# Ranks of layer 1's tokens from shifted products with the matrix of ones, without sums on GpSimd

## The reference, cut to what matters

```
def _L1_ffn_ref(x, gate_w, w1, w2, w3):
    xf = x.reshape(-1, orig_shape[-1])
    scores = jnp.einsum('td,ed->te', xf, gate_w)
    probs = jax.nn.softmax(scores.astype(jnp.float32), axis=-1)
    weights, idx = jax.lax.top_k(probs, TOP_K)          # TOP_K = 2 of 8
    weights = weights / jnp.sum(weights, axis=-1, keepdims=True)
    x1 = jax.nn.silu(jnp.einsum('td,efd->tef', xf, w1))
    x3 = jnp.einsum('td,efd->tef', xf, w3)
    out_all = jnp.einsum('tef,edf->ted', x1 * x3, w2)
    expert_outs = jnp.take_along_axis(out_all, idx[:, :, None], axis=1)
    result = jnp.einsum('tkd,tk->td', expert_outs, weights)
...
xn = _layernorm(x, axis=-1)
x = x + _L1_attn_ref(xn, ...) + _L1_ffn_ref(xn, L1_ffn_gate_w, L1_ffn_w1, L1_ffn_w2, L1_ffn_w3)
```

## Time and profile before

| | us |
|---|---|
| median of 3 runs | 1725.74 |
| lowest, highest | 1725.56, 1727.15 |
| span of the profiled execution (first to last instruction) | 1724.1 |
| TensorE busy in it | 1679.7 (97%) |
| VectorE, ScalarE, GpSimd busy | 1350.6, 812.6, 609.5 |

### The profile page before, as it was taken

The page is one execution under the profiler, slowest core; times in us unless marked ns, Lnnn a source line. Parts: engine busy times, 40 slices in busy tenths (PEclk is TensorE's granted clock), DMA queues, the critical chain, the costliest instruction groups (busy, mean ns, idle before and its releaser), DMA issues.

```text
span 1724.1 us, 24432 instructions
## 1 busy us (share of the span) xinstructions
PE 1679.7 (97%) x7020; PEld 1188.6 (69%) x7020; DVE 1350.6 (78%) x3866; ACT 812.6 (47%) x1456; POOL 609.5 (35%) x656
## 2 busy tenths in 40 slices
PE   5999999999999999999999999999999999999995
PEld 4667777777777777777777777777777766667773
DVE  5878888888888787979797979787888776565558
ACT  4535453636363545454544445454545343554431
POOL 3311242424242324233333232332323233567770
PEclk8999999999999999999999999999999999999998
DMA  8949474646373747373737373645546445577758
GB/s 211 201 104 256 100 187 105 178 109 181 99 181 101 182 103 194 97 200 86 202 84 192 85 189 90 174 106 135 144 106 167 99 109 154 191 266 266 237 173 312
DMA packets 172339, 273.89 MB, mean 159 GB/s; under 512 B 14312, under 2 KB 57320, under 8 KB 171952
## 3 DMA queue, kind: packets, MB, share of 16 engines
q1 hardware_dynamic: 163632, 254.63, 56.1%
q0 software_dynamic: 8576, 17.70, 3.2%
HBM read 202.15 MB, written 65.93 MB: 155 GB/s over the span
## 4 chain that ended last, share of the span: by engine, by line
PE 94%; DVE 2%; ACT 1%; issue 1%; DMA 1%; POOL 0%; SPq 0%; POOLq 0%; DVEq 0%; ACTq 0%
PE ps_y L709 26%; PE ps_gate L660 8%; PE ps_gate L661 8%; PE ps_gate L662 8%; PE ps_up L662 8%; PE ps_up L660 8%; PE ps_up L661 8%; PE ps_y L735 4%; PE ps_side L675 3%; PE ps_side L758 1%; PE ps_side L852 1%; PE ps_side L835 1%; PE ps_side L794 1%; PE ps_side L819 1%; PE ps_side L660 1%; PE ps_side L661 1%
## 5 line engine op out<-in xcount | busy, mean ns | idle before, releaser
L918 DVE TENSOR_TENSOR silu_h<-ps_up,silu_h 128x512 f32<-128x512 f32 x618 | 424.0, 686 | 295.3 <-ACT silu_h L1325 243.3
L1325 ACT ACTIVATE silu_h<-ps_gate 128x512 f32<-128x512 f32 x618 | 367.6, 598 | 567.4 <-PE ps_gate L662 565.1
L709 PE MATMUL ps_y<-silu_h,w_dn 128*128 128x512 f32 x1056 | 542.7, 595 | 3.0 <-DVE silu_h L912 3.0
L912 DVE TENSOR_TENSOR silu_h<-coef_b,silu_h 128x512 f32<-128x512 f32 x528 | 386.8, 732 | 13.0 <-DMA coef_b<-coef_kept 9.2
L660 PE MATMUL ps_gate<-xnT,w_gu 128*128 128x512 f32 x528 | 342.7, 649 | 0.0
L709 PEld LDWEIGHTS ps_y<-silu_h,w_dn 128*128 128x128 f32 x1056 | 199.7, 189 | 53.7 <-issue 7.7
L660 PE MATMUL ps_up<-xnT,w_gu 128*128 128x512 f32 x528 | 207.9, 394 | 4.6 <-DVE silu_h L918 4.6
L661 PE MATMUL ps_gate<-xnT,w_gu 128*128 128x512 f32 x528 | 209.4, 397 | 0.0
L662 PE MATMUL ps_gate<-xnT,w_gu 128*128 128x512 f32 x528 | 208.9, 396 | 0.0
L662 PE MATMUL ps_up<-xnT,w_gu 128*128 128x512 f32 x528 | 208.0, 394 | 0.0
L661 PE MATMUL ps_up<-xnT,w_gu 128*128 128x512 f32 x528 | 206.8, 392 | 0.0
(11 more groups left out here) (267 smaller groups left out, 2454.8 us busy)
## 6 DMA issues: line engine op xcount, KB each, us to landing
coef_b<-coef_kept SPq DMA_DIRECT2D x254, 512.0 KB, 6.8
slots_x<-empty SPq DMA_DIRECT2D x15, 2080.0 KB, 12.7
w_block<-w_kept SPq DMA_DIRECT2D x45, 512.0 KB, 3.9
xs<-slots_x SPq DMA_DIRECT2D x37, 260.0 KB, 3.8
y_back<-y_kept SPq DMA_DIRECT2D x15, 512.0 KB, 7.0
w_down<-in_ffn_w SPq DMA_DIRECT2D x45, 128.0 KB, 3.7
w_raw<-in_ffn_w SPq DMA_DIRECT2D x33, 128.0 KB, 7.9
xres<-in_x SPq DMA_DIRECT2D x16, 256.0 KB, 3.1
```

The costliest lines, as they stand in the source:

```text
L709: eng.matmul(ps_y[:, :], w_dn[:, j], silu_h[:, g % HBUFS], start=j == 0, stop=last).then_inc(pe_down)
L912: eng.tensor_tensor(silu_h[:, s], coef_b[:, q % COEF_RING, k], silu_h[:, s], ALU.mult).then_inc(dve_h)
L918: eng.tensor_tensor(silu_h[:, s], ps_up[g % 2][:, :], silu_h[:, s], ALU.mult).then_inc(dve_h1)
L1325: eng.activation(silu_h[:, s], ps_gate[g % 2][:, :], ACT.Silu).then_inc(act_silu)
```

## The change

"prefix" goes from both tables and from GpSimd, and `gbefore` and its semaphore `pool_before` with it. "rank" on TensorE now has five products in place of two: the one with `neg_before` as before, and four with `neg_ones`, each reading `gsel` from its first block on and writing the bank from block 1, 2, 3 and 4 on: 32, 24, 16 and 8 columns. What lands in a block is the sum over all blocks in front of it. "rank" no longer waits for GpSimd. "select" on VectorE, before it overwrites `gsel`, now waits until the "rank" of the chunk before has read it; GpSimd had that wait before, for `gbefore`.

```diff
@@ ROUTE1 and ROUTE1_LAST
-          (31, "prefix"), (39, "rank"), (40, "key"), ...
+          (39, "rank"), (40, "key"), ...
-               (16, "prefix"), (17, "rank"), (18, "key"), ...
+               (17, "rank"), (18, "key"), ...
@@ build_program
-        gbefore = sb("gbefore", [ROWS + 1, EXPERTS1])
@@ tensor, "rank"
                     eng.wait_ge(dve_sel, key + 1)
-                    eng.wait_ge(pool_before, (ROWS + 1) * (key + 1))
-                    eng.matmul(ps[:, 0:(ROWS + 1) * EXPERTS1], neg_before, flat(gsel[:, :, :]), start=True, stop=False)
-                    eng.matmul(ps[:, 0:(ROWS + 1) * EXPERTS1], neg_ones, flat(gbefore[:, :, :]), start=False, stop=True).then_inc(signal)
+                    wide = (ROWS + 1) * EXPERTS1
+                    eng.matmul(ps[:, 0:wide], neg_before, flat(gsel[:, :, :]), start=True, stop=False)
+                    for back in range(1, ROWS + 1):
+                        ins = eng.matmul(ps[:, back * EXPERTS1:wide], neg_ones, flat(gsel[:, 0:ROWS + 1 - back]), start=False, stop=back == ROWS)
+                    ins.then_inc(signal)
@@ vector, "select"
                     wait_own()
+                    if c > 0:
+                        eng.wait_ge(*done("rank", min(c, SPARSE) - 1))
                     eng.tensor_scalar(gsel[:, 0:ROWS], gleft[:, :, :], CHOSEN, None, ALU.is_le).then_inc(dve_sel)
@@ gpsimd
-                elif what == "prefix":
-                    ...
-                            eng.tensor_copy(gbefore[:, 1], gsel[:, 0]).then_inc(pool_before)
-                    ...
-                            eng.tensor_tensor(gbefore[:, r + 1], gbefore[:, r], gsel[:, r], ALU.add).then_inc(pool_before)
```

More of the change, by code:

```diff
@@ L78 @@
 ROUTE1 = [(5, "stats1"), (7, "norm1"), (8, "xT1"), (9, "x_lo1"), (10, "vl0"), (10, "vl1"), (11, "top1"), (12, "gate_exp"), (23, "softmax"), (30, "select"),
-          (31, "prefix"), (39, "rank"), (40, "key"), (41, "first2"), (42, "slot"), (43, "send0"), (45, "send1"), (47, "send2"), (48, "send3"),
+          (39, "rank"), (40, "key"), (41, "first2"), (42, "slot"), (43, "send0"), (45, "send1"), (47, "send2"), (48, "send3"),
           (49, "send4"), (51, "send5"), (53, "send6"), (54, "send7")]
 ROUTE1_LAST = [(5, "stats1"), (7, "norm1"), (8, "xT1"), (9, "x_lo1"), (10, "vl0"), (10, "vl1"), (11, "top1"), (12, "gate_exp"), (14, "softmax"), (15, "select"),
-               (16, "prefix"), (17, "rank"), (18, "key"), (19, "first2"), (20, "slot"), (20, "table"), (21, "send0"), (21, "send1"), (22, "send2"), (22, "send3"),
+               (17, "rank"), (18, "key"), (19, "first2"), (20, "slot"), (20, "table"), (21, "send0"), (21, "send1"), (22, "send2"), (22, "send3"),
                (23, "send4"), (23, "send5"), (24, "send6"), (24, "send7")]
@@ L363, in build_program @@
             sem(n) for n in ("act_kexp", "act_qexp", "act_qrelu", "dve_kfeat", "pool_qfeat"))
-        dve_gate, act_gate, dve_sel, dve_slot, dve_gw, dve_gates, pool_mark, pool_before, dve_logit1, dve_strike1, act_attend, dve_sum, act_keys = (
-            sem(n) for n in ("dve_gate", "act_gate", "dve_sel", "dve_slot", "dve_gw", "dve_gates", "pool_mark", "pool_before", "dve_logit1",
+        dve_gate, act_gate, dve_sel, dve_slot, dve_gw, dve_gates, pool_mark, dve_logit1, dve_strike1, act_attend, dve_sum, act_keys = (
+            sem(n) for n in ("dve_gate", "act_gate", "dve_sel", "dve_slot", "dve_gw", "dve_gates", "pool_mark", "dve_logit1",
                                  "dve_strike1", "act_attend", "dve_sum", "act_keys"))
@@ L1537, in step @@
                     eng.tensor_tensor(qf[:, :], qf[:, :], tmp0[:, :], ALU.add).then_inc(pool_qfeat)
-                elif what == "prefix":
[L1540 to L1548, removed]
-                            eng.tensor_copy(gbefore[:, 1], gsel[:, 0]).then_inc(pool_before)
-                        else:
-                            eng.wait_ge(pool_before, (ROWS + 1) * c + r + 1)
-                            eng.tensor_tensor(gbefore[:, r + 1], gbefore[:, r], gsel[:, r], ALU.add).then_inc(pool_before)
                 elif what.startswith("put"):
```

## The result

The changed kernel takes 1745.28 us (median of 4 runs, 1744.72 to 1745.75) where the kernel before takes 1725.86 (1725.56 to 1727.15): 19.4 us more, a ratio of 1.0112 with a 95% interval of 1.0100 to 1.0124. The prediction was 1735.1 us in a range of 1731 to 1739. The direction was right; the size was half of what came, outside the range.

A forecast was written before the change was run, and what follows sets the result against it. TensorE, busy 97% of the span, was taken as the bound: 9.9 us of added products less 0.5 us of wait gave +9.4 on 1724.1, 1733.5, plus 1.6 to the runs' median: 1735.1 us, range 1731 to 1739.

The forecast's parts named there:

- What bounds the kernel: At the ranks, TensorE alone is late, busy 893.00 of 893.00 us; anything between two tiles moves the end by its length.
- The price of the added products: At each rank on TensorE, three more float32 products of 0.22 us: 0.66 us, 9.9 us over 15 ranks.
- the rival in which a narrow product costs only its columns: At the ranks, 0.07 us more each, 1.0 us for 15, less 0.5: +0.5, 1726.2 us; chance 0.05.
- The wait at chunk 14: TensorE's rank at chunk 14 no longer waits for GpSimd's sums: 0.5 us come back, once.
- the rival that the wait was dearer than it is booked: 8.1 us of idle time before L825's weight loads goes too: +1.8 us, 1727.5 us; chance 0.04.
- GpSimd's sums and VectorE's wait at zero: Work leaving GpSimd gives nothing; VectorE's added wait before writing gsel has 66 us of slack and costs zero.
- The rival in which the sums hold VectorE back: GpSimd's 1.8 us of sums delay VectorE and TensorE follows: 27 us gained, 1708 us in all; chance 0.04.
- The stall behind chunk 14: After chunk 14's routing, VectorE waits 3.94 us for an indirect send, then TensorE waits; it moves with TensorE, giving nothing back.
- The clock: TensorE's clock falls near chunk 14's stall cost 3.4 us; as before 0.74, otherwise 0.13 (-3.4 to +3.4, 1731.7 to 1738.5 us).
- 9.9 - 0.5 = +9.4 us: Whole kernel: added products at 15 ranks less the wait at chunk 14, on the 1724.1 us span: 1733.5 us.
- a chunk longer by another amount with the same number of passes: Sign of being wrong: a full chunk grows by something other than 0.66 us though TensorE's passes are as forecast.

The follow-up runs named there:

- three_more: Kernel before, GpSimd's sums and places kept, plus three products with neg_ones at each rank into unread columns: 1786.96 us against 1777.38.
- ranks16: Changed kernel with 160 free bytes where gbefore stood and the five rank products in bfloat16: 1721.28 us against 1726.13, ratio 0.9973.
- kept_third: Changed kernel with 160 bytes per partition held free where gbefore stood, third run: 1735.41 us against 1725.98 for the kernel before, ratio 1.0056.
- keep_place: Changed kernel with 160 bytes per partition held free where gbefore stood, first run: 1785.32 us against 1777.38 for the kernel before.
- before16: Kernel before, GpSimd's sums and places kept, with its two rank products in bfloat16: 1721.84 us against 1726.13, ratio 0.9976.
- +64: ranks16 with 224 free bytes where gbefore stood, so w_gu and all behind 64 bytes higher than before the change: 1729.53 us against 1727.19.
- -64: ranks16 with 96 free bytes where gbefore stood, so w_gu and all behind 64 bytes lower than before the change: 1719.99 us against 1727.19.
- both_moved: Changed kernel with xnT to gsum, w_gu and all behind 32 bytes higher than before the change, distances kept: 1734.88 us against 1727.19.

## Why the prediction was right and wrong

**What bounds the kernel: right.** The 0.67 us that a rank takes more between two tiles stand whole in the distance from rank to rank, 90.04 against 89.37 us.

**The price of the added products: right.** 0.66 us a rank forecast, 0.67 measured, in the changed kernel and in three_more alone. The bound from 1 and 128 columns held for 8 to 32; the rival in which a narrow product costs only its columns is out for float32. The Trainium skill's page "TensorE: Matmul & The Clock Gate" (section "Back-to-back issue gap") gives about 81 ns for a pass at 128 columns; the float32 passes here take 110 ns. Its floor of about 25 ns for narrow products is met by the bfloat16 products of ranks16, 25 ns from start to start, and not by the float32 ones.

**The wait at chunk 14: right.** The idle time is gone. With all places kept the total is +9.4 us (kept_third, 6.9 to 12.6), as forecast; the rival that the wait was dearer than it is booked wanted +1.8 and is out with it.

**GpSimd's sums and VectorE's wait at zero: right.** keep_place and three_more have the same chunk, 90.04 us, without them and with them. The rival in which the sums hold VectorE back is out.

**The stall behind chunk 14: longer, and made up for elsewhere.** The prediction had it move with TensorE unchanged. TensorE's waits for `silu_h` there are 4.6 us before and 6.2 us after, out of these over the whole span:

```profile
PE ps_up L659 <- DVE silu_h L919: 6.6, 4, 4.3
```

The kernel of before16, in which GpSimd's sums stay, has 6.2 us there too, so their removal is not needed for it. Against that, two waits near the start are shorter, 5.1 and 2.1 us where they were 6.0 and 3.0. In kept_third it is much the same: the stall 1.5 us longer, the waits near the start 1.4 shorter, and the fall of the clock (0.83 in one stretch of ten us) costs 1.7 us where it cost 3.4. Each is one profiled execution. So it is partly luck that kept_third meets the sum to 0.1 us.

**The clock: as before.** It falls to 0.67 in one stretch of ten us and is 0.99 in the next, 3.4 us of full clock together, what it was in the earlier trace rows:

```profile
1440.00:1450.00 10.00, 5.71 (x14) 3.69 (x13) 8.46 (x26) 1.18 (x3) 4.90 (x4) 0.67 0.37 96
1450.00:1460.00 10.00, 10.00 (x49) 7.38 (x48) 5.99 (x11) 3.96 (x7) 4.39 (x6) 0.99 0.08 27
```

**The step that failed: the sum left out an edit.** "9.9 - 0.5 = +9.4 us" is the whole of what instructions do, and the diff also takes a tile out of SBUF. That was not priced at zero with a reason, it was not listed at all, nor were the instructions whose operands it shifts, six in each of 528 tiles. One sign of being wrong that the prediction named, a chunk longer by another amount with the same number of passes, is what came: 1.22 us where 0.66 was forecast. What the removed tile cost is the difference between the changed kernel and kept_third, 1745.28 - 1735.41 = 9.9 us: 0.55 us in each chunk, and about 1.2 us in the part behind the chunks (269.4 us from the first product of the units to the end, against 268.2 in kept_third and 268.1 before). The range took the clock in and had no case for it. The distance's role is shown, with `w_gu` as the partner by exclusion; what in the chip makes one distance better than another is not. The table has no simple rule in it, since +64 is bad, -64 good, and +64 and -64 are both multiples of 64. Which of the two operands waits for which cannot be read from these traces.

## What to carry to other kernels

Read the allocation in a diff as you read the instructions: a tile that is added, removed or resized moves all behind it, and where TensorE is the bound, 17 ns a tile were worth as much here as the work that the change was about. To judge an edit, keep the hole and measure the edit alone; then try a few distances between weights and streamed operand for their own sake. And before small exact integers are multiplied in float32, ask whether bfloat16 holds them: it made five products cheaper than two.

## What the runs showed of the hardware that I had not expected

- The distance in SBUF between the streamed operand and the weights of 512-column float32r products changes their durations by 2 to 6 ns each in five of six, up to 0.55 us in a chunk of 33 tiles. With the distance kept, both operands could stand 32 bytes higher at no cost (both_moved, 90.04 us).
- A bfloat16 product of 8 to 40 columns with its own 128x128 load costs about 25 ns in a row of such (ranks16); a float32 one costs 220 ns, whether it has 1, 8, 40 or 128 columns ("fold" and the ranks).
- The distance from rank to rank was the same to 0.01 us in repeated runs, even where the total differed by 50 us. That is how an effect of 17 ns a tile can be told from one profiled execution.
